# Six tiles kept across the blocks, their next contents loaded in the tail of the block before, and absent steps counted by the step ahead

## What is computed

```python
x = L0(x, ctx)   # cross attention, 32 query heads on 8 key heads, output product, residual, layer norm
x = L1(x, ctx)   # non-local block: softmax(phi^T theta) g(x), product Wz, batch norm over ALL sequences, + x
x = L2(x, ctx)   # RWKV-like: norm, shift, five low-rank mixes, decay scan over time with 32 heads of 16,
                 # group norm, gate, product Wo, residual; norm, shift, sigmoid(xr Wfr) * (relu(xk Wfk)^2 Wfv)
x = L3(x, ctx)   # layer:
h = x + softmax(min(q k^T / sqrt(32), mask)) v @ cproj_w + cproj_b     # q from norm1(x); k, v from ctx; 16 heads
out = h + gelu(norm2(h) @ fc_w + fc_b) @ proj_w + proj_b               # fc_w 512x2048, proj_w 2048x512
```

## Time and profile before

| | us |
|---|---|
| median of 3 runs | 4543.06 (4542.51 to 4543.21) |
| the profiled execution | 4538.07 |
| its span, first to last instruction | 4536.3 |
| mean granted TensorE clock over it | 0.966 of full |

### The profile page before, as it was taken

One profiled execution on the slowest core, in us unless ns is written; L12 is line 12 of the kernel. 1 busy time (PEld: TensorE's weight loads), 2 busy tenths in 40 slices (PEclk: granted clock), 3 DMA queues, 4 the chain that ended last, 5 costly groups with the idle time before them and its releaser, 6 DMA issues. The chain is left out here.

```text
span 4536.3 us, 78914 instructions
## 1 busy us (share of the span) xinstructions
PE 4181.0 (92%) x30432; PEld 2555.1 (56%) x30432; DVE 2301.8 (51%) x2689; ACT 1501.9 (33%) x2558; POOL 1418.3 (31%) x1181
## 2 busy tenths in 40 slices
PE   7999999995889999999999998689999999999998
PEld 5666666662566666666666665344454444544443
DVE  4565656663466666666666665253333333433330
ACT  2545454553233333334333333112122222212220
POOL 2333333331454445444444443021111111111110
PEclk9999999997889999999999998899999999999999
DMA  3112121112100000100000100210000000000000
GB/s 98 59 58 69 54 65 57 64 42 85 60 16 25 25 25 27 35 26 25 25 25 25 34 15 10 99 73 1 29 1 29 18 12 29 1 29 1 29 10 10
DMA packets 102633, 161.24 MB, mean 36 GB/s; under 512 B 17232, under 2 KB 34768, under 8 KB 101808
## 3 DMA queue, kind: packets, MB, share of 16 engines
q1 hardware_dynamic: 102320, 156.39, 10.1%
HBM read 106.00 MB, written 41.94 MB: 33 GB/s over the span
## 5 line engine op out<-in xcount | busy, mean ns | idle before, releaser
L1375 DVE COPY_PREDICATED b_A<-b_mask,b_pS 128x2048 f32<-128x2048 uint32 x128 | 458.1, 3579 | 213.9 <-PE b_pS L1102 213.4
L1761 PE MATMUL c_pR<-c_xT,c_fc_w 128*128 128x512 f32 x1024 | 460.3, 597 | 7.3 <-PEq L1666 2.4
L1827 PE MATMUL c_pR<-c_proj_w,c_fcT 128*128 128x512 f32 x1024 | 459.5, 597 | 7.5 <-ACTq L1666 3.8
L695 POOL TENSOR_TENSOR a_S<-a_S,a_negmax 128x2048 f32<-128x2048 f32 x64 | 231.1, 3610 | 560.3 <-DVE a_negmax L629 560.3
L1102 PE MATMUL b_pS<-b_R,b_kT 32*128 32x128 f32 x7168 | 274.0, 290 | 80.8 <-POOL b_kT L1532 34.9
L1528 POOL TENSOR_TENSOR b_R<-b_R,b_Wh 128x512 f32<-128x512 f32 x192 | 226.3, 1178 | 376.9 <-PE b_pS L1102 376.5
L1978 POOL TENSOR_TENSOR c_S<-c_S,c_negmax 128x1024 f32<-128x1024 f32 x64 | 121.4, 1897 | 701.3 <-DVE c_negmax L1925 701.3
L1951 DVE TENSOR_TENSOR c_res<-c_res,c_pR 128x512 f32<-128x512 f32 x128 | 88.0, 687 | 482.8 <-PE c_pR L1827 449.4
L1761 PEld LDWEIGHTS c_pR<-c_xT,c_fc_w 128*128 128x128 f32 x1024 | 192.2, 191 | 245.8 <-issue 242.0
L1102 PEld LDWEIGHTS b_pS<-b_R,b_kT 32*128 32x128 f32 x7168 | 230.1, 191 | 171.5 <-issue 91.7
L1827 PEld LDWEIGHTS c_pR<-c_proj_w,c_fcT 128*128 128x128 f32 x1024 | 189.7, 190 | 238.4 <-issue 228.0
(11 more groups left out here) (224 smaller groups left out, 8012.0 us busy)
## 6 DMA issues: line engine op xcount, KB each, us to landing
a_c<-ctx SPq DMA_DIRECT2D x16, 512.0 KB, 3.7
a_x<-x SPq DMA_DIRECT2D x16, 512.0 KB, 4.7
a_kexp<-a_kT SPq DMA_DIRECT2D x512, 16.0 KB, 1.8
a_xl<-x SPq DMA_DIRECT2D x32, 256.0 KB, 2.6
a_cl<-ctx SPq DMA_DIRECT2D x32, 256.0 KB, 2.9
mid_x<-a_xl SPq DMA_DIRECT2D x32, 256.0 KB, 2.9
mid_wy<-a_wy SPq DMA_DIRECT2D x32, 256.0 KB, 2.1
b_x1g<-mid_x SPq DMA_DIRECT2D x16, 512.0 KB, 4.1
```

What stands on the lines that cost most here:

```text
L695: nc.gpsimd.tensor_tensor(S[n % 2][:, :, :], S[n % 2][:, :, :], negmax[n % 2][:, :].unsqueeze(2).to_broadcast([P, RH, T]), ALU.add)\
L1375: nc.vector.copy_predicated(A[:, :, :].rearrange("p q (n two h) -> p q n two h", two=2, h=h)[:, :, :, 1, :], masks[h][:, :].bitcast(U32).r ...
L1761: mm = nc.tensor.matmul(bank, w[:, c, at * P:at * P + P], src[:, c, :], start=(c == 0), stop=(c == KC - 1))
L1827: mm = nc.tensor.matmul(bank, fcT[part % 2][:, m, g * T:g * T + T], proj_w[:, KC * part + m, :], start=(m == 0), stop=(m == KC - 1))
```

## The change

- ident, vec (all of its columns), Wk, Wv, Wr and a tile rows of 4x512 columns are allocated in program, ahead of all phases; Wg behind phase_a. phase_b's x1g and wyg become the two halves of rows; phase_c's c_xn becomes rows, and its k_w, q_w, v_w, cproj_w lie in Wk, Wr, Wv, Wg.
- In phase_a, behind turn N - 2 of the tail, SyncE issues Wk, Wv, Wr and the first rows of x1 and wy for phase_b. phase_b no longer loads these, nor vec and ident; y_loaded is counted by SyncE. In phase_b, behind turn N, it issues the context of phase_c's group 0 and the four weights into the kept tiles, each behind a wait for its last product. Each phase waits for the end of these loads before it ends.
- In phase_c loaded_k and loaded_att are gone; GpSimd and VectorE wait for rows (loaded_rows) alone. c_loaded is counted by SyncE.
- In phase_c skip is gone. An absent item is added to the count by the last present item ahead of it of the same counter (step_of), or at the head of a turn by lead; and fill, in the first and the last turn, waits for the last present item of the same bank. phase_a and phase_b keep skip.

The diff, cut: edits that only put kept tiles or filled(...), empty(...) in the old names' places are left out.

```diff
-def phase_a(nc, dram, stats):
+KEPT = {"ident": [P, P], "vec": [P, KC * (len(VECS) - 2 + 4 + 5)], "Wk": [P, KC, D], "Wv": [P, KC, D], "Wr": [P, KC, D], "rows": [P, 4, D]}
+def phase_a(nc, dram, stats, kept):
@@ -186,8 +189,8 @@
...
+        bk, ci, bz = sb("bk", [P, 1]), sb("ci", [2 * CI, 2]), sb("bz", [P, 1])
+        rows, ident, vec = sb("rows", [P, 3 * D + P + CI]), kept["ident"], kept["vec"]
@@ -370,7 +373,7 @@
                 part = slice(h * CI, h * CI + CI)
                 for dst, name in [(wthT[:, part], "L1_WthetaT"), (wphT[:, part], "L1_WphiT"), (wzT[part, :], "L1_WzT"), (ci[part, :], "L1_ci")]:
                     sp.dma_start(dst, dram[name]).then_inc(*loaded_rest.up(16))
-            sp.dma_start(vec[:, :], dram["vecs"][:, 0:KC]).then_inc(*loaded_rest.up(16))
+            sp.dma_start(vec[:, :], dram["vecs"]).then_inc(*loaded_rest.up(16))
             for i in (-1, 0, 1):
                 turn(Turn(None, add=i), i % 2, True)
             with sp.Fori(0, (N - 4) // 2) as reg:
@@ -378,6 +381,12 @@
                     turn(Turn(reg, 2, 2 + u), u, False)
             for i in range(N - 2, N + 2):
                 turn(Turn(None, add=i), i % 2, True)
+                if i == N - 2:
+                    for n in ("Wk", "Wv", "Wr"):
+                        sp.dma_start(kept[n][:, :, :], dram["L2_%sT" % n].rearrange("(k p) n -> p k n", p=P)).then_inc(*loaded_next.up(16))
+                    for at, name in ((0, "x1"), (G, "wy")):
+                        sp.dma_start(kept["rows"][:, at:at + G, :], dram[name].rearrange("b t d -> t b d")[:, 0:G, :]).then_inc(*loaded_next.up(16))
+            sp.wait_ge(loaded_next.sem, loaded_next.seen)
             for g in range(G):
                 sp.wait_ge(*x1_stored[g](N - 1, 16))
                 sp.wait_ge(*wy_stored[g](N - 1, 16))
@@ -783,11 +792,10 @@
...
-        W = {n: sb("w" + n, [P, KC, D]) for n in ("Wk", "Wv", "Wr", "Wg", "Wo", "Wfk", "Wfr", "Wfv")}
+        W = {n: kept[n] if n in kept else sb("w" + n, [P, KC, D]) for n in ("Wk", "Wv", "Wr", "Wg", "Wo", "Wfk", "Wfr", "Wfv")}
...
-        vec = sb("vec", [P, dram["vecs"].shape[1]])
-        ident, heads, parity = sb("ident", [P, P]), sb("heads", [P, HC]), sb("parity", [P, 2])
+        ident, vec, heads, parity = kept["ident"], kept["vec"], sb("heads", [P, HC]), sb("parity", [P, 2])
...
+        x1g, wyg, x2 = kept["rows"][:, 0:G, :], kept["rows"][:, G:2 * G, :], sb("x2", [P, G, D])
@@ -943,10 +952,11 @@
                         .then_inc(*stored.up(16))
 
 
-            for tile, name in [(vec, "vecs"), (ident, "ident"), (heads, "heads"), (parity, "parity")]:
+            for n in range(2):
+                sp.sem_inc(*y_loaded.up(16))
+            for tile, name in [(heads, "heads"), (parity, "parity")]:
                 sp.dma_start(tile[:, :], dram[name]).then_inc(*loaded_w.up(16))
             sp.dma_start(state[:, :, :, :], dram["state_rows"]).then_inc(*loaded_w.up(16))
-            load(Turn(None))
             load_state(Turn(None), 0)
             load_state(Turn(None, add=1), 1)
 
@@ -957,10 +967,8 @@
             w2 = dram["L2_xattn_maa_w2"].rearrange("f d e -> (f d) e")
             for tile, src in [(w2a, w2[0:4 * DM, :]), (w2b, w2[4 * DM:5 * DM, :]), (td2, dram["L2_xattn_td_w2"])]:
                 sp.dma_start(tile[:, :], src).then_inc(*loaded_k.up(16))
-            load_weights(loaded_k, W["Wk"], "L2_WkT")
             load_weights(loaded_v, td1, "L2_xattn_td_w1")
-            for signal, n in [(loaded_v, "Wv"), (loaded_v, "Wr"), (loaded_v, "Wg"), (loaded_f, "Wo"), (loaded_f, "Wfk"), (loaded_f, "Wfr"),
-                              (loaded_f, "Wfv")]:
+            for signal, n in [(loaded_v, "Wg"), (loaded_f, "Wo"), (loaded_f, "Wfk"), (loaded_f, "Wfr"), (loaded_f, "Wfv")]:
                 load_weights(signal, W[n], "L2_%sT" % n)
@@ -984,6 +992,16 @@
                     turn(Turn(reg, 2, 2 + u), u, False)
             for i in range(N - 2, N + 2):
                 turn(Turn(None, add=i), i % 2, True)
+                if i == N:
+                    last = Turn(None, add=N - 1)
+                    wait(x2_saved.all(last))
+                    wait(xn_ready[0].all(last))
+                    wait(R_.full(last, "w", 1))
+                    sp.dma_start(kept["rows"][:, :, :], dram["ctx_2048"].rearrange("b t d -> t b d")[:, 0:2 * G, :]).then_inc(*loaded_next.up(16))
+                    for n, name, behind in [("Wk", "k_w", ("k", 1)), ("Wr", "q_w", ("r", 1)), ("Wv", "v_w", ("v", 1)), ("Wg", "cproj_w", ("g", 1))]:
+                        wait(R_.full(last, *behind))
+                        sp.dma_start(W[n][:, :, :], dram["L3_xattn_" + name].rearrange("(k p) n -> p k n", p=P)).then_inc(*loaded_next.up(16))
+            sp.wait_ge(loaded_next.sem, loaded_next.seen)
             sp.wait_ge(*stored.all(Turn(None, add=N - 1)))
@@ -1587,13 +1604,12 @@
...
+        W = {"k_w": kept["Wk"], "q_w": kept["Wr"], "v_w": kept["Wv"], "cproj_w": kept["Wg"]}
...
+        rows, ident, vec = sb("rows", [P, 3 * D]), kept["ident"], kept["vec"]
...
+        x, res, c_xn = sb("x", [P, G, D]), sb("res", [P, G, D]), kept["rows"]
@@ -1639,32 +1655,46 @@
...
-        def run(eng, step, skip):
+        def there(t, n):
+            return 0 <= t - 1 + LAG[items[n][0][0]] < NG
+        def step_of(signal, who, j, name):
+            at, n, more = when(j, name), ring.at[name], 0
+            if at.reg is None:
+                while n + more + 1 < len(items) and not (ring.who[n + more + 1] in who and there(at.add, n + more + 1)):
+                    more += 1
+                more = [w in who for w in ring.who[n + 1:n + 1 + more]].count(True)
+            return signal.up(1 + more)
+        def filled(j, *name):
+            return step_of(ring.filled, ("act", "dve"), j, name)
+        def empty(who, j, *name):
+            return step_of(emptied[who], (who,), j, name)
+        def run(eng, step, signal=None, who=()):
+            def lead(i):
+                mine = [n for n, w in enumerate(ring.who) if w in who]
+                first = [there(i.add + 1, n) for n in mine].index(True) if mine else 0
+                if first:
+                    eng.wait_ge(signal.sem, (i.add + 2) * signal.per)
+                    eng.sem_inc(*signal.up(first))
 
             def turn(i, static):
+                if static:
+                    lead(i)
                 for s in TABLE:
                     if not static or 0 <= i.add + LAG[s] < NG:
                         step(i + LAG[s], s, int(s[1:]) if s[1:].isdigit() else 0)
-                    else:
-                        skip(i + 1, s)
 
             turn(Turn(None, add=-1), True)
             with eng.Fori(0, NG - 1) as reg:
                 turn(Turn(reg), False)
             turn(Turn(None, add=NG - 1), True)
-        def skipped(eng, who):
-            def skip(at, s):
-                mine = [name for name, w in ITEMS[s] if who in (None, w)]
-                if mine:
-                    n = ring.at[mine[0]]
-                    for name in mine if who is None else ():
-                        for free in ring.ready(at, name):
-                            eng.wait_ge(*free)
-                    eng.wait_ge(*(ring.filled(at, n) if who is None else emptied[who](at, ring.nth[n] - 1)))
-                    eng.sem_inc(*(ring.filled if who is None else emptied[who]).up(len(mine)))
-            return skip
 
@@ -1710,17 +1740,11 @@
...
-            sp.dma_start(ident[:, :], dram["ident"]).then_inc(*loaded_k.up(16))
-            load_context(Turn(None))
-            weight(loaded_k, W["k_w"], "k_w")
+            sp.sem_inc(*c_loaded.up(16))
             for g in range(G):
                 load_rows(Turn(None), g)
-            sp.dma_start(vec[:, :], dram["vecs"][:, VEC0:]).then_inc(*loaded_k.up(16))
-            weight(loaded_att, W["q_w"], "q_w")
             load_mask(Turn(None))
-            weight(loaded_att, W["v_w"], "v_w")
-            sp.dma_start(rows[:, :], dram["rows_c"]).then_inc(*loaded_att.up(16))
-            weight(loaded_att, W["cproj_w"], "cproj_w")
+            sp.dma_start(rows[:, :], dram["rows_c"]).then_inc(*loaded_rows.up(16))
             weight(loaded_mlp, fc_w, "fc_w")
             weight(loaded_mlp, proj_w, "proj_w")
...
 
...
-            pe.wait_ge(loaded_k.sem, loaded_k.seen)
...
                 at, n = when(j, name), ring.at[name] - RING
-                last = {ring.who[n]: (at if n >= 0 else at + -1, ring.nth[n])}
+                if at.reg is None:
+                    while at.add * len(items) + n >= 0 and not there(*divmod(at.add * len(items) + n, len(items))):
+                        n -= RING
+                    turns, n = divmod(n, len(items))
+                    last = {ring.who[n]: (at + turns, ring.nth[n])}
+                else:
+                    last = {ring.who[n]: (at if n >= 0 else at + -1, ring.nth[n])}
...
-                    mm.then_inc(*ring.filled.up())
+                    mm.then_inc(*filled(j, s, c))
...
```

(51 more changed lines are left out.)

23 lines of the change are left out of this document (10 added, 13 removed).

## The result

The changed kernel takes 4505.54 us, the median of four runs (4501.56 to 4511.13), against 4543.14 of the kernel before in the same series (4542.51 to 4545.05): a ratio of 0.9916, 95% interval 0.9901 to 0.9931. Its profiled execution took 4507.38 with a span of 4504.7, at a granted clock of 0.968 (before: 4538.07, 4536.3, 0.966).

A forecast was written before the change was run, and what follows sets the result against it. TensorE, busy 92% of the span, was taken as the bound. Gains of 0.8 (phase_b entry), 13.7 (phase_c entry), 9.7 (last turn) and 2.0 (first turn) sum to 26.2 us: 4543.06 becomes 4516.9, range 4508 to 4526.8.

The forecast's parts named there:

- What bounds the kernel, and where: TensorE, busy 92% of the span; phase_c's looped turns full, idle only at both block entries and the last turn.
- Entry of phase_b: Wait before phase_b's first matmul: ended by VectorE's constants, not the loaded rows; gain 0.8 us, bounds 0 and 1.2.
- Entry of phase_c: Head of phase_c: earlier TensorE start brings n1 13.7 us sooner, bounds 6.9 and 15, keeping the transposes' slow start.
- Loads where they go: Tails of phase_a and phase_b: the moved loads, 4.2 and 5.2 MB, delay later transfers but lose nothing.
- The 0 for vec: phase_a: loading vec at 54 KB instead of 2 costs TensorE 0, bounds -0.5 and +0.3 us.
- Skipped steps: phase_c without skips: last turn gains 9.7 us (bounds 7 and 11), first turn 2.0 (bounds 0 and 4).
- The median's 5.0 us over the profiled run: Whole kernel: median of runs stands 5.0 us above the profiled execution, left unchanged when forecasting the new median.
- 1: Head of phase_c: rows_c lands late, GpSimd holds n1, which gains 6.9 us, not 13.7: 4523.7; chance 0.10.
- 2: Start of phase_c: TensorE's code is fetched behind loads of x, starting it 4.7 us later: 4521.6; chance 0.06.
- 3: Last turn of phase_c: gaps come from bank waits, not skips, and stay; gain 16.5 us, 4526.6; chance 0.07.
- 4: phase_a's tail: early loads hold back pair 15's xl, making the kernel slower, 4552; chance 0.02.
- 5: Two losses at once, or half-clock stretches falling worse in phase_b and first turns: gain under 9.1, about 4536; chance 0.04.

The follow-up runs named there:

- the kernel with this part alone: Kernel before with only phase_b's tiles kept and loaded early in phase_a's tail, phase_c as before: 4533.35 us, ratio 0.9986.
- the kernel with counts alone: Kernel before with phase_c's skips replaced by counts, no load moved: 4527.15 us, ratio 0.9972.

## Why the prediction was right and wrong

- **What bounds the kernel, and where:** right. The loop from its third product on is the same to 0.02 us.
- **Entry of phase_b:** what ends the wait and the 0.8 us (found 0.84) were right; what they are worth was not. This is the step that failed. It says "Gain 0.8 us, bounds 0 and 1.2", as if a shift of all that follows had no other price, and the sum leaves phase_b's 1788 us at nothing. The shift moved phase_b to another place against the clock's changes. That was worth 5.2 us in the first pair of traces and 5.9 by the means of two each; the kernel with this part alone gained 4.8 in all by the medians and 6.4 by the ratio (interval 2 to 10).
- **Entry of phase_c:** 13.3 for 13.7. TensorE started 1.89 us into the block for 1.65; rows_c landed 9.7 us into it for 8.35. The kept slow start was right here: the transposes took 3.67 us. Part of this closeness is the draw of the traces: in the second trace of the changed kernel k0 and k1 ran at a granted clock of 0.80, 8.82 us in place of 7.13, and n1 came 13.19 us behind TensorE's start and not 11.50. The gain between the second traces is 12.9.
- **Loads where they go:** right, in both tails. The 0 for vec: TensorE waited 2.72 us in place of 2.07, 0.65 us where the bound was 0.3, and yet phase_a's later work started 0.3 us sooner; that phase_a ended 2 us later in this trace is the spread from run to run. Its first 120 us were 5.2 us longer, at a granted clock of 0.86 in place of 0.97; VectorE's seventh reduction of the scores starts anywhere from 119.5 to 125.0 us in the fourteen traces, and at 125.0 in one of the kernel before with a delay. The tail gave 4 back. The last statistics stand at 1097.8 to 1103.2 in the six traces of the old phase_a and at 1096.2 to 1105.3 in the eight of the new one.
- **Skipped steps:** right to 0.1 us in the last turn, 9.7. In the first turn 2.0 was forecast and 2.0 came in the kernel with counts alone; F0 and F1 at full clock, 2.1 more, had not been foreseen: the sum has the head of the loop at nothing too.
- **The median's 5.0 us over the profiled run:** it was taken from three runs. All 79 runs of the kernel before, in five series on more than one chip, have the mean 4540.5 (4530.9 to 4548.3), and nine of the changed kernel 4506.1: 34.4 us. The sum of the table, with the first pair of traces and without phase_a, is 33.6. So some 3 us of the 37.6 are the sample. Worked out from 4540.5, the range would have begun near 4505.5, at the measured time; the mechanism would have been as incomplete.
- **Rivals:** 1 was near, since GpSimd did wait for rows_c, but not long enough. 2 didn't happen: TensorE started 1.89 us into the block, ahead of the first load's landing, so it didn't wait for code behind the loads. The Trainium skill, Runtime: NRT & Kernel Launch, section Instruction fetch mechanics, says that a taken branch outside the loaded pages waits for a DMA to fetch the code; the start of this block shows no such wait. 3 and 4 didn't happen. In 5 stood "stretches at half clock that fall worse in phase_b and the first turns": the mechanism, but with the loss alone. It works both ways, and here it gave 7.3 us. That the shift fell on a good place and not on a bad one is luck. The range's low end had only the upper bounds of the costed gains, and missed by 2.5.

Open: why phase_a's end gathers at one place while its start does not; what in the stretch ahead decides whether the clock falls; and how much of phase_b's length beyond the spot goes with the place, since each place has one trace. Single runs of one kernel spread over 10 us and more.

## What to carry to other kernels

A sum of gains is not the gain when TensorE's clock changes in the course of a kernel: a shift of a microsecond ahead of a phase with short waits was worth 6 us here, and with 1.2 us more it was lost again. Look in such a phase for half-clock stretches right behind a short wait (the clock column of the busy time by stretch), put as much into both ends of the range, and test with a delay in an idle spot; a delay that costs nothing, or far more than its length, shows it. The first three runs of before agreed within 0.7 us and stood 2.5 us above its mean; with ten runs of each kernel the intervals here were 0.1% to either side, so a gain of 0.3% wants that many.

## What the runs showed of the hardware

- All changes of the granted clock in a trace lie whole numbers of one equal step apart (to 0.005 us), and the program's start doesn't set where (0.05 to 2.63 us into a step). Yet by the end of phase_a twelve of fourteen executions stand within 0.3 us of each other in it.
- phase_b lasts 1782.0 to 1791.1 us by the place of its first matmul; between places 1.01 and 1.20 it changes by 6 us.
- A stretch of 10.24 us at half clock, full of matmuls, stood behind a wait of 2.30 us in the kernel before and was absent behind one of 1.64 us in the changed one; the stretch around it took 5.4 us longer.
- 0.8 MB that were issued behind 1.1 MB landed in 5.5 and 6.4 us in the two traces of the changed kernel, behind 5 MB in 12.3.
